# RMSNorm mean squares from two float32r matmuls on split sums instead of one float32 matmul

## The reference

```
y   = clip(modulated 1x1 convolution of x)             # per sample styles
h   = y * rsqrt(mean(y*y) + 1e-6) * norm_w             # first mean square
gate, hs, r, i = four 512x512 products of h            # gelu, -, sigmoid, sigmoid
a   = exp(-8 softplus(alpha) r);  s = sqrt(1 - a*a) * hs * i
out = scan over time: o = a*o + s
hs2 = out * gate + y
h2  = hs2 * rsqrt(mean(hs2*hs2) + 1e-6) * norm2_w      # second mean square
x  += (f2(h2) * gelu(g2(h2))) @ out_w.T + out_b + hs2  # width 1536
```

## Time and profile before

| | |
|---|---|
| median of 3 runs | 1876.88 us (1875.87 to 1877.12) |
| profiled execution | 1877.14 us, span 1875.1 us |
| PE busy | 1836.8 us (98%) |
| VectorE, ScalarE, GpSimd busy | 1003.1, 762.0, 391.5 us |
| mean granted clock of PE | 0.993 |
| mean squares | 8 in attention, 8 in MLP, one float32 matmul each |

### The profile page before, as it was taken

One profiled execution on the slowest core, in us unless ns is written; L12 is line 12 of the kernel. 1 busy time (PEld: TensorE's weight loads), 2 busy tenths in 40 slices (PEclk: granted clock), 3 DMA queues, 4 the chain that ended last, 5 costly groups with the idle time before them and its releaser, 6 DMA issues.

```text
span 1875.1 us, 23560 instructions
## 1 busy us (share of the span) xinstructions
PE 1836.8 (98%) x8374; PEld 1486.3 (79%) x8374; DVE 1003.1 (53%) x1651; ACT 762.0 (41%) x1154; POOL 391.5 (21%) x345
## 2 busy tenths in 40 slices
PE   7999999999999999999999999999899999999996
PEld 6788888888888888888888888877687787788774
DVE  6656666647743333333242423437875776676665
ACT  6655555556532222121222222234454644544543
POOL 0022222112100000000000000004454654564433
PEclk9999999999999999999999999999999999999998
DMA  5011110013401010101001010534122122222201
GB/s 193 1 45 46 45 45 24 23 45 115 177 1 68 1 67 1 69 1 67 1 24 45 1 68 1 180 139 158 36 69 103 52 84 92 66 70 91 67 12 46
DMA packets 55185, 114.07 MB, mean 61 GB/s; under 512 B 4226, under 2 KB 4482, under 8 KB 55092
## 3 DMA queue, kind: packets, MB, share of 16 engines
q1 hardware_dynamic: 49956, 95.00, 14.6%
q0 software_dynamic: 4608, 16.78, 2.8%
q10 hardware_dynamic: 528, 1.05, 0.2%
HBM read 87.65 MB, written 25.17 MB: 60 GB/s over the span
## 4 chain that ended last, share of the span: by engine, by line
PE 94%; DVE 2%; issue 1%; ACT 0%; DMA 0%; POOL 0%; DVEq 0%; SPq 0%; ACTq 0%
PE bank L810 28%; PE bank L284 18%; PE bank L825 14%; PE bank L1436 13%; PE bank L1454 5%; PE bank L1472 5%; PE bank L270 3%; PE bank L1384 2%; PE bank L1393 2%; PE bank L1400 1%; PE bank L839 1%; PE bank L1389 0%; DMA x_tiles<-x_d 0%; PE bank L1441 0%; PE bank L796 0%
## 5 line engine op out<-in xcount | busy, mean ns | idle before, releaser
L284 PE MATMUL bank<-h_parts,gate_w 128*128 128x512 f32 x1536 | 355.9, 393 | 0.1
L284 PEld LDWEIGHTS bank<-h_parts,gate_w 128*128 128x128 f32 x1536 | 289.4, 188 | 64.4 <-issue 4.4
L1020 DVE SCALAR_TENSOR_TENSOR product_full<-bank,vec_sb,gelu 128x512 f32<-128x512 f32 x96 | 72.0, 750 | 425.0 <-PE bank L810 375.5
L1436 PE MATMUL bank<-operand_parts,int_w 128*128 128x512 f32 x1152 | 281.7, 391 | 2.0 <-DVE operand_parts L1957 2.0
L825 PE MATMUL bank<-mlp_out_w,product_parts 128*128 128x512 f32 x1152 | 283.5, 395 | 0.0
L810 PE MATMUL bank<-h_parts,mlp_gate_w 128*128 128x512 f32 x1152 | 276.9, 389 | 1.2 <-DVE h_parts L1005 1.2
L810 PE MATMUL bank<-h_parts,mlp_fc_w 128*128 128x512 f32 x1152 | 276.8, 389 | 0.0
L825 PEld LDWEIGHTS bank<-mlp_out_w,product_parts 128*128 128x128 f32 x1152 | 214.0, 188 | 51.9 <-issue 6.7
L1436 PEld LDWEIGHTS bank<-operand_parts,int_w 128*128 128x128 f32 x1152 | 216.2, 188 | 47.3 <-issue 3.0
L810 PEld LDWEIGHTS bank<-h_parts,mlp_gate_w 128*128 128x128 f32 x1152 | 216.1, 188 | 46.8 <-issue 2.0
L810 PEld LDWEIGHTS bank<-h_parts,mlp_fc_w 128*128 128x128 f32 x1152 | 216.2, 188 | 44.9
(11 more groups left out here) (256 smaller groups left out, 2311.7 us busy)
## 6 DMA issues: line engine op xcount, KB each, us to landing
xin<-xT SPq DMA_DIRECT2D x8, 1024.0 KB, 7.0
hs_d<-u SPq DMA_DIRECT2D x8, 1024.0 KB, 5.1
x_tiles<-x SPq DMA_DIRECT2D x8, 1024.0 KB, 5.5
x_d<-x_tiles SPq DMA_DIRECT2D x8, 1024.0 KB, 4.4
x_tiles<-x_d SPq DMA_DIRECT2D x8, 1024.0 KB, 5.8
out<-u_tiles SPq DMA_DIRECT2D x32, 256.0 KB, 2.0
raw_w<-int_W SPq DMA_DIRECT2D x7, 1024.0 KB, 8.4
x_residual<-x_d SPq DMA_DIRECT2D x28, 256.0 KB, 2.9
```

Source lines behind the costliest of these rows:

```text
L284: i = pe.matmul(bank[:], gw[:, w, s, k, m * P:(m + 1) * P], hr[:, q, t, k, :], start=k == 0 and n == 0, stop=k == KT - 1 and n == 2)
L1020: dve.scalar_tensor_tensor(out=pf[:], in0=FB[j % 2][:], scalar=v("mlp_fc_b", j), in1=gg[:], op0=ALU.add, op1=ALU.mult).then_inc(p_full, 1)
L1436: i = pe.matmul(A[m][:], w1[OPER[o]][:, a, k, m * P:(m + 1) * P], op[:, s % 4, c, :], start=s == 0 and n == 0, stop=False)
```

## The change

The matrix of 1/512 is now of type float32r (`ones_r`, filled by a VectorE copy from a scratch tile in setup). After `add_squares`, ScalarE copies the sum into a float32r high part (`sum_high`) and VectorE subtracts it from the sum for the low part (`sum_low`); PE waits for both (`sq_high`, `sq_low`) and does two float32r matmuls that accumulate in the bank. In attention the parts lie in the first tile of block b + 1's half of `h_parts`, in the MLP in `square_sum_parts`, over two tiles of `h2_full`. Attention's blocks 0 and 1 keep one float32 matmul (`mean_square_early`). In the attention body, the two steps stand behind `x_parts(b + 2)` and `x_low_part(b + 2)`, and before `decay(b, q, 0)` and `tile(b, q, 0)`. For the MLP's first block `sum_high(0)` stands behind `split_high(0)`.

```diff
--- before.py
+++ after.py
@@ -64,7 +64,7 @@
         ps = [ctx.enter_context(nc.psum_tensor(f"bank{i}", [P, 512], F32)) for i in range(8)]
         vec = ctx.enter_context(nc.sbuf_tensor("vec_sb", [P, NVEC], F32))
         ident = ctx.enter_context(nc.sbuf_tensor("ident_sb", [P, P], F32))
-        ones = ctx.enter_context(nc.sbuf_tensor("ones_mean", [P, P], F32))
+        ones_r = ctx.enter_context(nc.sbuf_tensor("ones_mean", [P, P], F32R))
         eps6 = ctx.enter_context(nc.sbuf_tensor("eps6", [P, 8], F32))[:, 0:1]
 
         def v(name, k=None):
@@ -79,10 +79,10 @@
             return nc.alloc_sbuf_tensor_at(name, shape, dt, offset=base + where)
 
         def following(sems, marks):
-            return mlp_half(nc, at, sems, marks, ps, vec, v, ident, ones, eps6, ins, x_nat, hs2_d, x1_d, out_v)
+            return mlp_half(nc, at, sems, marks, ps, vec, v, ident, ones_r, eps6, ins, x_nat, hs2_d, x1_d, out_v)
 
         with nc.Block() as block:
-            attention_half(nc, block, following, ps, vec, v, ident, ones, eps6, ins, xT, hs2_d)
+            attention_half(nc, block, following, ps, vec, v, ident, ones_r, eps6, ins, xT, hs2_d)
 
 
 def two_ahead(eng, first, body):
@@ -121,7 +121,7 @@
     return tokens[:, bass.ds(n, 1), :].rearrange("p n c -> p (n c)")
 
 
-def attention_half(nc, block, following, ps, vec, v, ident, ones, eps6, ins, xT, hs2_d):
+def attention_half(nc, block, following, ps, vec, v, ident, ones_r, eps6, ins, xT, hs2_d):
 
     sems = []
     mem = ExitStack()
@@ -188,6 +188,7 @@
         x_loaded, x_high, x_low = sem("x_loaded"), sem("x_high"), sem("x_low")
         y_ps, y_evac, y_clip, y_sq = sem("y_ps"), sem("y_evac"), sem("y_clipped"), sem("y_squared")
         cur_done = sem("cur_tab_done")
+        sq_high, sq_low = sem("sq_sum_high"), sem("sq_sum_low")
         sq_add, ms_ps, rms, rinv = sem("sq_added"), sem("mean_sq_ps"), sem("rms_done"), sem("rstd_done")
         h_full, h_high, h_low = sem("h_full_done"), sem("h_high"), sem("h_low")
         hs_ps, r_ps, i_ps, g_ps = sem("hs_ps"), sem("r_ps"), sem("i_ps"), sem("gate_ps")
@@ -271,9 +272,15 @@
                                           start=k == 0 and n == 0, stop=k == KT - 1 and n == 2)
                     i.then_inc(y_ps, 1)
 
-            def mean_square(b, dst=C[0]):
+            def mean_square_early(b, dst):
                 pe.wait_ge(sq_add, 3 * (b + 1))
-                pe.matmul(dst[:], ones[:], hf[:, 0, :], start=True, stop=True).then_inc(ms_ps, 1)
+                pe.matmul(dst[:], ones_r[:].bitcast(F32), hf[:, 0, :], start=True, stop=True).then_inc(ms_ps, 1)
+
+            def mean_square(b, q):
+                pe.wait_ge(sq_high, b - 1)
+                pe.wait_ge(sq_low, b - 1)
+                pe.matmul(C[0][:], ones_r[:], hr[:, q, 0, 0, :], start=True, stop=False)
+                pe.matmul(C[0][:], ones_r[:], hr[:, q, 1, 0, :], start=False, stop=True).then_inc(ms_ps, 1)
 
             def product(q, bank, w, m, done, first=False):
                 for k in range(KT):
@@ -314,8 +321,10 @@
                 if nxt and not (isinstance(b, int) and b == 0):
                     project(b + 1)
                 gates(b, q, 0)
-                if nxt:
-                    mean_square(b + 1)
+                if isinstance(b, int) and b == 0:
+                    mean_square_early(1, C[0])
+                elif nxt:
+                    mean_square(b + 1, 1 - q)
                 for m in range(1, KT):
                     if not nxt and m == 2:
                         early()
@@ -350,7 +359,7 @@
                         pe.wait_ge(y_evac, KT + m - 1)
                     project_early(1, m)
                     if m == 0:
-                        mean_square(0, MS0)
+                        mean_square_early(0, MS0)
 
             two_ahead(pe, prepare, body)
             run()
@@ -380,6 +389,11 @@
                 for m in range(KT):
                     act.wait_ge(y_clip, KT * b + m + 1)
                     act.activation(hf[:, m, :], y[:, q, m, :], ACT.Square).then_inc(y_sq, 1)
+
+            def sum_high(b, q):
+                act.wait_ge(g_ps, KT * (b - 1))
+                act.wait_ge(sq_add, 3 * (b + 1))
+                act.activation(hr[:, q, 0, 0, :], hf[:, 0, :], ACT.Copy).then_inc(sq_high, 1)
 
             def root(b):
                 act.wait_ge(ms_ps, b + 1)
@@ -418,6 +432,8 @@
                     squares(b + 1, 1 - q)
                 if nxt2:
                     x_parts(b + 2, q)
+                if nxt and not (isinstance(b, int) and b == 0):
+                    sum_high(b + 1, 1 - q)
                 decay(b, q, 0)
                 if nxt:
                     root(b + 1)
@@ -553,6 +569,11 @@
                 dve.wait_ge(sq_add, 3 * b + 2)
                 dve.tensor_tensor(hf[:, 0, :], hf[:, 0, :], hf[:, 2, :], ALU.add).then_inc(sq_add, 1)
 
+            def sum_low(b, q):
+                dve.wait_ge(sq_add, 3 * (b + 1))
+                dve.wait_ge(sq_high, b - 1)
+                dve.tensor_tensor(hr[:, q, 1, 0, :], hf[:, 0, :], hr[:, q, 0, 0, :].bitcast(F32), ALU.subtract).then_inc(sq_low, 1)
+
             def normalise(b, q):
                 dve.wait_ge(rms, b + 1)
                 dve.reciprocal(rstd[:], rstd[:]).then_inc(rinv, 1)
@@ -585,6 +606,8 @@
                     add_squares(b + 1)
                 if nxt2:
                     x_low_part(b + 2, q)
+                if nxt and not (isinstance(b, int) and b == 0):
+                    sum_low(b + 1, 1 - q)
                 tile(b, q, 0)
                 if nxt:
                     normalise(b + 1, 1 - q)
@@ -634,8 +657,9 @@
                 dve.memset(mhalf, -0.5)
                 dve.memset(quarter, 0.25)
                 dve.memset(eps6, 1e-6)
-                dve.memset(ones[:], 1.0 / D)
+                dve.memset(tr[:, 0:P], 1.0 / D)
                 link(dve.memset(keep[:], 1.0))
+                dve.tensor_copy(ones_r[:], tr[:, 0:P])
                 for s in range(BATCH):
                     dve.memset(keep[:, s * BPB:s * BPB + 1], 0.0)
                 link(dve.memset(so[:], 0.0))
@@ -681,7 +705,7 @@
             run()
 
 
-def mlp_half(nc, at, sems, att, ps, vec, v, ident, ones, eps6, ins, x_nat, hs2_d, x1_d, out_v):
+def mlp_half(nc, at, sems, att, ps, vec, v, ident, ones_r, eps6, ins, x_nat, hs2_d, x1_d, out_v):
 
     def sem(name):
         return nc.alloc_semaphore(name)
@@ -692,6 +716,7 @@
     ow = [at(f"mlp_out_w{n}", [P, 2, KT, D], w, F32R) for n, w in enumerate((O0, O1, O2))]
     z = [at("hs2_even", [P, KT, BT], Z0), at("hs2_odd", [P, KT, BT], Z1)]
     hf = at("h2_full", [P, KT, BT], HF_AT)
+    su = at("square_sum_parts", [P, 2, BT], HF_AT + 2 * KB, F32R)
     hr = at("h2_parts", [P, 2, KT, BT], HR_AT, F32R)
     gg = at("gelu2", [P, BT], GG_AT)
     pf = at("product_full", [P, BT], PF_AT)
@@ -715,6 +740,7 @@
     z_loaded = (sem("hs2_loaded0"), sem("hs2_loaded1"))
     sq_done, sq_add, ms_ps, rms, rinv = (sem("hs2_squared"), sem("sq2_added"), sem("mean_sq2_ps"),
                                          sem("rms2_done"), sem("rstd2_done"))
+    sq_high, sq_low = sem("sq2_sum_high"), sem("sq2_sum_low")
     h_full, h_high, h_low = sem("h2_full_done"), sem("h2_high"), sem("h2_low")
     g_ps, f_ps, g_evac, p_full = sem("mlp_gate_ps"), sem("mlp_fc_ps"), sem("gelu2_done"), sem("p_full_done")
     p_high, p_low, o_ps, t_ps = sem("p_high"), sem("p_low"), sem("mlp_out_ps"), sem("hs2_tok_ps")
@@ -792,8 +818,10 @@
         last_early, ready, tokens, last_run = ffn["tensor"](pe, last_of, FB)
 
         def mean_square(b, bank):
-            pe.wait_ge(sq_add, 3 * (b + 1))
-            pe.matmul(bank[:], ones[:], hf[:, 0, :], start=True, stop=True).then_inc(ms_ps, 1)
+            pe.wait_ge(sq_high, b + 1)
+            pe.wait_ge(sq_low, b + 1)
+            pe.matmul(bank[:], ones_r[:], su[:, 0, :], start=True, stop=False)
+            pe.matmul(bank[:], ones_r[:], su[:, 1, :], start=False, stop=True).then_inc(ms_ps, 1)
 
         def wait_weights(b, n):
             if isinstance(b, int) and b == 0:
@@ -907,6 +935,10 @@
             for k in range(KT):
                 act.activation(hf[:, k, :], z[q][:, k, :], ACT.Square).then_inc(sq_done, 1)
 
+        def sum_high(b):
+            act.wait_ge(sq_add, 3 * (b + 1))
+            act.activation(su[:, 0, :], hf[:, 0, :], ACT.Copy).then_inc(sq_high, 1)
+
         def root(b):
             act.wait_ge(ms_ps, b + 1)
             if not (isinstance(b, int) and b == 0):
@@ -934,6 +966,8 @@
                     split_high(NEXT + j)
                 if nxt and j == SQ:
                     squares(b + 1, 1 - q)
+                if nxt and j == SQ + 1:
+                    sum_high(b + 1)
                 if nxt and j == MS - 1:
                     root(b + 1)
                 if not nxt:
@@ -946,6 +980,7 @@
                 act.wait_ge(att["projected"], KT * NB)
                 squares(0, 0)
                 split_high(0)
+                sum_high(0)
             elif m == 1:
```

(8 more changed lines are left out.)

## The result

| | before | changed |
|---|---|---|
| median of 10 runs | 1876.97 us (1875.87 to 1880.63) | 1883.43 us (1881.47 to 1885.04) |
| ratio, 95% interval | | 1.0033 (1.0024 to 1.0042) |
| profiled execution, span | 1877.14, 1875.1 | 1882.94, 1880.9 |

The change makes the kernel slower by 0.33%, 6.2 us by the ratio. The forecast was 1882.5, slower by 0.3%, in a range of 1879.2 to 1885.4.

What follows compares the result with a forecast made beforehand. PE, busy for 98% of the span, bounds the kernel. Attention stalls +5.3, block 6 -0.45, first MLP mean square +2.2, other seven -3.15, clock +1.7 sum to +5.6 us: 1882.5 by the median, range 1879.2 to 1885.4.

Steps and rivals of the forecast that it cites:

- Five stalls in attention: Attention blocks 1 to 5: PE stalls 1.39 us before each changed mean square, net +1.06 each, +5.3 us in all.
- DVE, not ACT, is last: Attention block 1: sum_high on ACT is done at 114.33, sum_low on DVE only at 115.34.
- The first mean square of the MLP: Inside attention block 7: PE stalls 2.63 us until sum_low is done, net +2.2 us.
- The gain of a mean square: At each changed mean square: two float32r matmuls (0.45 us) replace 0.90 us of PE time, gaining 0.45 without waiting.
- No cost at the MLP's other seven, nor in setup: MLP blocks 1 to 7: parts ready before PE comes, 7 x -0.45 = -3.15 us; the setup copy costs nothing.
- The clock at the long stall: Before the MLP's first mean square: PE's 2.47 us of idling drops the clock to half once, +1.7 us.
- rival A: The clock doesn't fall at the 2.5 us stall before the MLP's first mean square: +3.9 us, 1880.8; chance 30%.
- B: Faster: the parts reach PE in time in attention and at the MLP's start, 6.4 us gained, 1870.5; chance 6%.
- C: Attention's five short stalls drop the clock as well: five times 1.7 us more, 1891.0; chance 6%.
- D: The new matmuls run no faster than half a float32 one: 6.3 us more, 1888.8; chance 2%.
- the chance of "slower": Probability given that the whole change measures as slower, with the line at 1880.6 us: 0.71.

Runs made afterwards that it cites:

- attn_no_low: Changed kernel without the low part of the sum in attention, one float32r matmul instead of two for blocks 2 to 7: 1875.11 against 1876.44 us before, ratio 0.9991.
- two_sum_low: Changed kernel with attention's low-part subtraction issued twice on VectorE: 1889.09 us against 1876.63 for the kernel before, ratio 1.0068.
- after: The changed kernel itself, its profiled execution, against the kernel before: median 1883.43 against 1876.97 us, ratio 1.0033.
- mlp_only: Only the MLP has the change, attention keeps float32 mean squares: 1878.37 us, ratio 1.0012 against the kernel before.
- pad_after: Changed kernel with 16 one-column memsets more at the start of VectorE's setup: 1882.42 us, ratio 1.0032 against the kernel before.
- attn_only: Only attention (blocks 2 to 7) has the change, the MLP keeps float32 mean squares: 1882.02 against 1876.44 us for the kernel before, ratio 1.0029.
- inside_gates: As sums_first, but PE does the MLP's first mean square 12 matmuls later, inside gates(7, 2): 1871.92 us, ratio 0.9975 against the kernel before.
- sums_first: Changed kernel with sum_high ahead of x_parts and split_high(0), sum_low ahead of the x_low subtractions: 1873.48 against 1876.44 us before, ratio 0.9984.
- first_f32: As sums_first, but the MLP's first mean square is one float32 matmul without sum_high and sum_low: 1872.01 against 1876.58 us before, ratio 0.9973.

## Why the prediction was right, point by point

- **Five stalls in attention.** Forecast: 1.39 us and PE idle for 1.23; the trace has 1.45 (114.78 less 113.33, where the step after the last product would be) and 1.30. The hand-over from DVE took 0.14 and not 0.08. Net 1.11 a block for 1.06.
- **DVE, not ACT, is last**: shown from both sides by attn_no_low and two_sum_low.
- **The first mean square of the MLP**: stall 2.72 for 2.63, idle 2.56 for 2.47, net 2.27 for 2.2.
- **The gain of a mean square** was sized a little high, 0.45 against 0.41. I had put all of the uneven steps behind the mean square down to the float32 type; the products after the new matmuls run unevenly as well. For the eight mean squares without a stall this is 0.3 us.
- **No cost at the MLP's other seven, nor in setup**: no wait there in the trace.
- **The clock at the long stall was the weak step.** I took one fall for certain (+1.7). It did not happen in the profiled execution of the changed kernel:

```profile
447.00:450.40 3.40, 0.84 (x5) 0.41 (x4) 1.19 (x2) 3.40 (x7) 0.00 (x0) 1.00 0.36 130
450.40:453.90 3.50, 3.50 (x16) 2.90 (x17) 3.35 (x5) 3.47 (x6) 1.48 (x1) 1.00 0.00 0
```

Of the five traces with this stall (after, mlp_only, attn_no_low, pad_after, two_sum_low) two have the fall (mlp_only and pad_after), 1.6 us each. So rival A's case and the forecast's both occur. What my sum lacked and the trace has in place of it is 1.9 us in the last stage, 1.1 of them VectorE's pauses. The total came right partly by luck, these two errors having about the same size: stalls and gains alone make 5 x 1.11 - 0.41 + 2.27 - 7 x 0.41 = +4.5 us, the pauses 1.1, and the clock 0.6 to 0.7 on average of the five traces. That is 6.2 to 6.3, beside 6.2 measured; it leaves out the other 0.8 us of the last stage and the 0.4 us given back at the MLP's loop start, so the agreement to 0.1 us is no proof of each term.
- **Rivals B, C and D** fell: B's price, though, was right as a remedy. Parts in time give 1871.9, with 1870.5 forecast. C needed a fall behind 1.3 us of idling; none of 15 such stalls (after, attn_only, pad_after) has one. D needed matmuls of half a float32 one, 0.45 us each; they start 0.23 us apart where PE doesn't wait.
- **Two slips that change nothing in the sum.** All fourteen changed mean squares lie between 60 and 1150 us, not twelve (the last is at 1138). And the chance of "slower" adds up to at least 0.48 + 0.17 + 0.06 + 0.02 = 0.73, not 0.71.

## What to carry to other kernels

When one engine is busy for 98% of the time, operands that a cheaper instruction needs must be queued on the other engines ahead of work that nobody waits for yet: the same 28 added steps made this kernel 0.33% slower in one order and 0.25% faster in another (inside_gates). Before putting a step into a queue, write down the time at which its input is ready, at which its engine gets to it and at which its reader comes; here each was in the trace of before to within 0.1 us. Where the operand can't be ready in time, move the reader behind other work of its own, or leave that one instance in the dear form.

## What the runs showed of the hardware that I had not expected

- The fall of the clock behind one and the same gap is a matter of the execution. Behind PE's waits of 2.5 us (before attention block 1's mean square in twelve traces, before the MLP's in five) it fell 9 times in 17; behind 1.9 us 3 times in 6 (the five stalls of two_sum_low, and the wait before 1313.70 in the changed kernel, without a fall); behind 1.3 us never in 15. Where two such waits follow each other (2.3 us and 2.2 to 2.9 us, in the last stage) it fell in all twelve. In attn_only, for one, the clock stayed at 2.4 GHz behind the wait that cost the kernel before 1.7 us:

```profile
54.50:57.40 2.90, 0.43 (x3) 0.02 (x1) 2.06 (x4) 0.77 (x2) 0.00 (x0) 1.00 0.00 0
58.00:61.50 3.50, 3.50 (x16) 2.74 (x15) 2.74 (x4) 3.47 (x6) 0.00 (x0) 1.00 0.02 5
```

By the Trainium skill (TensorE: Matmul & The Clock Gate, "HAM oscillation — how this bites in real kernels") only longer gaps bite; these runs disagree, down to 1.9 us. Its section "What's actually happening" says that the window over which activity is watched is free-running and doesn't start with the kernel, so that the same kernel can differ from run to run; the 9 of 17 agree with that. One trace is no proof that a gap of this size costs or doesn't.
- A pause of VectorE of 0.35 us, once in each pass of a loop, stands at another instruction when the number of instructions ahead in its program changes, in a stage that no edit touches. It costs nothing where VectorE would idle next, and 3 x 0.35 us where PE waits for the following step (after, sums_first, inside_gates, first_f32). A difference of 1 us between two versions of this kernel can be that alone.
